# Projections of the local attentions: a reordered pipeline, the rotation's sum on GpSimd, one pipeline over both rows

## The chip, the cores and the metric

The kernel runs on one core of a Trainium2 chip. The metric is the device time of one execution in microseconds (us). A core has five engines that run their own instruction streams: TensorE (PE in the profile; its weight loads are PEld), VectorE (DVE), ScalarE (ACT), GpSimd (POOL), and SyncE (SP), which here only issues DMAs. They meet through semaphores. PSUM is what TensorE writes its sums to; SBUF is the on-chip memory that all engines read.

## The reference

Two transformer blocks over a batch of 2 rows of 2048 tokens with 256 features. The change touches one step of the last part, which runs twice (two layers). Cut to that step:

```
h = shift_token(x)                      # 4096 x 256: half of the features from the token before
q, k, v = split(h @ wqkv, 3)            # 256 x 1536
q = l2norm(q) * qs ; k = l2norm(k) * ks # per head, 8 heads of 64
q, k = rotary_xpos(q, k)                # q * cos*scale + rotate_half(q) * sin*scale, k with 1/scale
o = local_attention(q, k, v)            # windows of 128 tokens
```

The local attention and a gated unit follow; they aren't changed.

## The kernel before

The whole network is one program of stages with a barrier of all engines between them. `local_projections` (names I_... in the profile) is one such stage and runs twice. It takes the 32 tiles of 128 tokens (16 per row, `WIN` = 16, `B` = 2 rows) one after the other; u = tile mod 2 picks one of two buffers. For one tile n:

- SyncE loads the tile's tokens into `h` (two DMAs: the shifted half, L1553, and the other, L1554).
- *first*: TensorE transposes `h` into the PSUM tile `ph` (L1584). ScalarE copies `ph`, rounded, into `hhi` (L1625) and VectorE takes the rest, `hlo = ph - hhi` (L1679). Three products of such halves stand for one product in float32. `ph` is a single buffer.
- *mul*: TensorE does 18 matmuls (L1595): 12 into `pqk[u]` (q and k), then 6 into `pv`. ScalarE squares q and k (L1631, tile `sq`), copies v out (L1636) and takes the root of the sums (L1639). VectorE sums the squares (L1700, `ss`), clips the norm from below (L1707, on `nr`), inverts it (L1708, `rn`) and writes the normalised `qn` (L1709). SyncE stores v.
- *rotation*: GpSimd makes `t2`, the half with the sine, in two instructions of 128x512 (L1655). VectorE makes `t1 = qn * A` (L1687) and adds `t2` to it (L1691). `A` and `R` are tables (cosine and sine parts times the scale), made once at the start of the stage.
- *turn*: TensorE transposes the 128x1024 result in 8 pieces into `pt` (L1610), ScalarE copies that to `tT` (L1644), SyncE stores q and k (L1566).

Each engine's order is written out by hand in `skewed`: per row, tile n+1's *first* is issued inside tile n's *mul*, *turn* runs two tiles behind. VectorE rotates tile n-1 between the sum of squares and the clip of tile n. The loop `Fori(0, B)` runs the pipeline once per row, so it drains at the end of row 0 and fills again.

At the stage's start SyncE loads weights, tables, scales and an identity, in this order, then the first tokens. Everything waits for all four.

The views of the profile leave out buffer numbers, so `t1` and `t2` both read as I_t: L1655 writes t2, L1687 and L1691 write t1.

Of the kernel before, what the change touches and what calls it, by code (L numbers as in the profile page):

```python
# [1476 lines left out]
def local_projections(nc, sem, tag, xp, wqkv, tab, scales, ident, qT, kT, ve):  # L1477
# [5 lines left out]
    H = LD // 2  # L1483
    with ExitStack() as ctx:
# [36 lines left out]
        def skewed(eng, first, mul, turn):  # L1521


            M = WIN // 2
            with eng.Fori(0, B) as b:
                first(b, 0, 0, 0)
                mul(b, 0, 0, 0, (b, 1, 0, 1))
                mul(b, 1, 0, 1, (b, 2, 1, 0))
                with eng.Fori(0, M - 2) as m:
                    for u in range(2):  # L1530
                        mul(b, m * 2 + u + 2, m + 1, u, (b, m * 2 + u + 3, m + 1 + u, 1 - u))
                        turn(b, m * 2 + u, m, u)
                mul(b, WIN - 2, M - 1, 0, (b, WIN - 1, M - 1, 1))
                turn(b, WIN - 4, M - 2, 0)
                mul(b, WIN - 1, M - 1, 1, None)
                turn(b, WIN - 3, M - 2, 1)
                turn(b, WIN - 2, M - 1, 0)
                turn(b, WIN - 1, M - 1, 1)

        def nothing(*a):  # L1540
            pass

        @block.sync
        def _(sp):
            sp.dma_start(w[:], wqkv.rearrange("(kc p) n -> p kc n", p=P)).then_inc(c_in, 16)
            sp.dma_start(tb[:], tab.rearrange("(k w p) d -> p k w d", p=P, w=WIN)).then_inc(c_in, 16)
            sp.dma_start(sc[:].rearrange("p k d -> p (k d)"), scales.to_broadcast([P, 2 * LD])).then_inc(c_in, 16)
            sp.dma_start(idf[:], ident).then_inc(c_in, 16)

            def first(b, w_, m, u):  # L1550
                sp.wait_ge(t_done, b * WIN + w_ + 1)
                row = b * PADS + w_ * P
# [3 lines left out]
            def mul(b, w_, m, u, nxt):  # L1556
                if nxt:
                    first(*nxt)
                sp.wait_ge(v_done, b * WIN + w_ + 2)
                sp.dma_start(ve[ds(b * PADW + w_ * P + P, P), :], v[:, u].rearrange("p h e -> p (h e)")  # L1560
                             ).then_inc(v_out[u], 16)
# [6 lines left out]
            skewed(sp, first, mul, turn)  # L1568
# [5 lines left out]
        def _(pe):  # L1574
            for s in (t_done, v_mm, qt_done):
                pe.sem_inc(s, 1)
            pe.wait_ge(c_in, 64)
            pe.wait_ge(wlo_done, 2)

            def first(b, w_, m, u):  # L1580
                pe.wait_ge(h_in[u], b * (WIN // 2 * 32) + m * 32 + 32)
                pe.wait_ge(ht_done, b * WIN + w_ + 1)
# [4 lines left out]
            def mul(b, w_, m, u, nxt):  # L1587
                n = b * WIN + w_
# [12 lines left out]
                if nxt:  # L1601
                    first(*nxt)

            def turn(b, w_, m, u):
                n = b * WIN + w_
# [7 lines left out]
            skewed(pe, first, mul, turn)  # L1613

        @block.scalar
        def _(act):
            act.wait_ge(v_set, 2)
            act.wait_ge(c_in, 64)
            act.activation(whi[:], w[:], ACT.Copy).then_inc(whi_done, 1)

# [6 lines left out]
            def mul(b, w_, m, u, nxt):  # L1627
                n = b * WIN + w_
# [12 lines left out]
            def turn(b, w_, m, u):  # L1641
                act.wait_ge(qt_done, b * WIN + w_ + 3)
                act.wait_ge(qk_out[u], b * (WIN // 2 * 32) + m * 32 + 1)
                act.activation(tT[:, u].rearrange("p j g t -> p j (g t)"), pt[:], ACT.Copy).then_inc(ev_done, 1)  # L1644
            skewed(act, first, mul, turn)

        @block.gpsimd
        def _(pool):
            pool.wait_ge(tabs, 2)

            def mul(b, w_, m, u, nxt):

                pool.wait_ge(qn_done, b * WIN + w_ + 3)
# [5 lines left out]
            skewed(pool, nothing, mul, nothing)  # L1659

        @block.vector
        def _(dve):
            dve.wait_ge(c_in, 64)
            dve.sem_inc(qn_done, 1)
            dve.memset(v[:], 1.0).then_inc(v_set, 1)
            for j in range(2):
                dve.tensor_tensor(A[:, j], tb[:, 2 * j], sc[:, j:j + 1].to_broadcast([P, WIN, LD]), ALU.mult)
                for a, z in ((0, H), (H, 0)):
                    last = dve.tensor_tensor(R[:, j, :, a:a + H], tb[:, 2 * j + 1, :, a:a + H],
                                             sc[:, j:j + 1, z:z + H].to_broadcast([P, WIN, H]), ALU.mult)  # L1670
            last.then_inc(tabs, 1)
            dve.wait_ge(whi_done, 2)
            dve.tensor_tensor(wlo[:], w[:], whi[:].bitcast(F32), ALU.subtract).then_inc(wlo_done, 1)
            dve.wait_ge(tabs, 2)

            def first(b, w_, m, u):
                n = b * WIN + w_
# [19 lines left out]
            def mul(b, w_, m, u, nxt):  # L1697
                n = b * WIN + w_
# [736 lines left out]
```

## Time and profile before

| | us |
|---|---|
| median of 3 runs | 5195.83 |
| lowest, highest | 5181.3, 5202.37 |
| the profiled execution | 5158.03 |
| its span, first to last instruction | 5156.5 |
| the first of the two stages, first DMA issue to last | about 275 (3283 to 3558) |
| the second | about 280 (4199 to 4479) |

The span is 1.5 us under the time of the same execution. All durations below are from this one execution. A row of a timeline gives start, duration, engine, line, operation, output and inputs, and in brackets how long the engine had been idle and what released it. A duration includes any time in which the instruction was held by something inside the engine.

### The profile page before, as it was taken

The numbers are of one execution on the slowest core, as the hardware profiler recorded it, in microseconds if no ns is written. First come the engines' busy times: TensorE is split into PE (matmuls) and PEld (weight loads), VectorE is DVE, ScalarE is ACT, GpSimd is POOL, SyncE is SP. The second block draws the span as 40 slices with busy tenths as digits, with TensorE's granted clock in tenths as the row PEclk, the third lists the DMA queues.
The fourth block names the chain that finished last, engine by engine and source line by source line (L and its number), as shares of the span: only waits on it lengthen the run. The fifth ranks groups of instructions, "written<-read, shape, count | busy, mean of one in ns | idle before, by whom it ended". The sixth has DMA issues, their size and how long they took to land. (4 is left out here: it accounts for less than half of the span.)

```text
span 5156.5 us, 83448 instructions
## 1 busy us (share of the span) xinstructions
PE 4120.5 (80%) x25572; PEld 2739.7 (53%) x25572; DVE 3024.9 (59%) x5338; ACT 2489.3 (48%) x4335; POOL 1363.3 (26%) x2120
## 2 busy tenths in 40 slices
PE   4799999753999994659999996576996967699687
PEld 2444444343999992324444442454665755466465
DVE  1788878441444543748878783575563447656454
ACT  1377767612545541217767675233553423355343
POOL 1232323124000005011111111133882003388300
PEclk9699989976999997858979898798998989899898
DMA  7322322123121203361422221334451023444211
GB/s 227 40 33 33 51 35 33 45 101 108 49 88 49 70 31 119 123 115 26 64 43 45 43 45 64 109 120 142 155 156 51 28 57 115 147 148 156 73 37 37
DMA packets 327112, 413.90 MB, mean 80 GB/s; under 512 B 40772, under 2 KB 236225, under 8 KB 323196
## 3 DMA queue, kind: packets, MB, share of 16 engines
q1 hardware_dynamic: 278620, 257.43, 15.8%
q0 software_dynamic: 43552, 148.12, 13.5%
q8 instruction: 174, 2.85, 0.2%
q10 hardware_dynamic: 4608, 4.20, 0.2%
q14 instruction: 158, 1.29, 0.1%
HBM read 252.57 MB, written 156.19 MB: 79 GB/s over the span
## 5 line engine op out<-in xcount | busy, mean ns | idle before, releaser
L600 DVE TENSOR_REDUCE G_mpart<-G_pm 128x1 f32<-128x512 f32 (+3 forms) x1024 | 618.4, 651 | 209.6 <-PE G_pm L489 202.2
L600 DVE TENSOR_REDUCE B_mpart<-B_pm 128x1 f32<-128x512 f32 (+3 forms) x1024 | 618.1, 651 | 157.3 <-PE B_pm L489 149.3
L579 ACT ACTIVATE G_p<-G_psc 128x1024 f32<-128x1024 f32 (+1 forms) x576 | 532.9, 977 | 151.7 <-PE G_psc L526 149.9
L579 ACT ACTIVATE B_p<-B_psc 128x1024 f32<-128x1024 f32 (+1 forms) x576 | 532.2, 977 | 134.6 <-PE B_psc L526 132.8
L489 PE MATMUL G_pm<-G_ks,G_qs 48*128 48x512 f32 (+3 forms) x1664 | 466.3, 425 | 100.3 <-DMA G_ks<-G_one 58.4
L489 PE MATMUL B_pm<-B_ks,B_qs 48*128 48x512 f32 (+3 forms) x1664 | 453.7, 410 | 74.8 <-DMA B_ks<-B_one 42.5
L489 PEld LDWEIGHTS G_pm<-G_ks,G_qs 48*128 48x128 f32 x1664 | 253.0, 212 | 421.3 <-DVE G_mpart L600 210.7
L1786 POOL TENSOR_SCALAR J_pr<-J_pr,J_rc 128x256 f32<-128x256 f32 x512 | 462.8, 916 | 39.9 <-DVE J_rc L1924 37.5
L489 PEld LDWEIGHTS B_pm<-B_ks,B_qs 48*128 48x128 f32 x1664 | 241.8, 200 | 386.2 <-DVE B_mpart L600 218.7
L504 PE MATMUL G_po<-G_p,G_v 128*32 128x512 f32 (+3 forms) x2560 | 326.6, 592 | 0.1
L526 PE MATMUL G_psc<-G_qs,G_ks 50*128 50x512 f32 (+3 forms) x1280 | 307.0, 418 | 9.3 <-issue 6.8
L504 PE MATMUL B_po<-B_p,B_v 128*32 128x512 f32 (+3 forms) x2560 | 306.5, 562 | 1.2 <-POOL B_p L356 1.1
L1655 POOL TENSOR_TENSOR I_t<-I_qn,I_R 128x512 f32<-128x512 f32 x128 | 165.8, 1316 | 513.6 <-DVE I_qn L1709 513.6
L526 PE MATMUL B_psc<-B_qs,B_ks 50*128 50x512 f32 (+3 forms) x1280 | 292.3, 402 | 9.4 <-issue 6.8
L1141 ACT ACTIVATE E_hs<-E_pH,E_bf 128x384 f32<-128x384 f32 (+1 forms) x192 | 115.8, 603 | 346.6 <-PE E_pG L1094 346.3
L1094 PE MATMUL E_pH<-E_xT,E_wfg 128*128 128x384 f32 (+1 forms) x1152 | 252.5, 355 | 25.6 <-DVE E_wfg L1180 18.7
L1885 ACT ACTIVATE J_pr<-J_pS,J_nm 128x256 f32<-128x256 f32 x512 | 235.3, 479 | 38.0 <-DVE J_nm L1920 38.0
L1094 PE MATMUL E_pG<-E_xT,E_wfg 128*128 128x384 f32 (+1 forms) x1152 | 249.4, 352 | 0.0
L1107 PE MATMUL E_pO<-E_wp,E_a 128*128 128x256 f32 (+1 forms) x1920 | 234.6, 283 | 0.0
L1094 PEld LDWEIGHTS E_pH<-E_xT,E_wfg 128*128 128x128 f32 x1152 | 210.9, 191 | 36.5 <-issue 26.2
L1107 PEld LDWEIGHTS E_pO<-E_wp,E_a 128*128 128x128 f32 (+1 forms) x1920 | 230.0, 184 | 0.0
L1185 DVE SCALAR_TENSOR_TENSOR E_z<-E_pG,E_bg,E_hs 128x384 f32<-128x384 f32 (+1 forms) x192 | 123.6, 644 | 165.9 <-ACT E_hs L1141 164.8
(303 smaller groups left out, 7895.3 us busy)
## 6 DMA issues: line engine op xcount, KB each, us to landing
J_v<-lve SPq DMA_DIRECT2D x64, 520.0 KB, 3.8
J_k<-lkT SPq DMA_DIRECT2D x64, 512.0 KB, 4.9
lve<-I_v SPq DMA_DIRECT2D x64, 260.0 KB, 2.1
lqT<-I_tT SPq DMA_DIRECT2D x64, 256.0 KB, 2.4
lkT<-I_tT SPq DMA_DIRECT2D x64, 256.0 KB, 2.6
J_q<-lqT SPq DMA_DIRECT2D x64, 256.0 KB, 3.8
ein<-Z_z SPq DMA_DIRECT2D x8, 1228.0 KB
E_xin<-ein POOLq DMA_DIRECT2D x8, 1152.0 KB, 6.2
```

Of the source, the lines that this page charges most:

```text
L489: last = pe.matmul(t[:, n * w:(n + 1) * w], qs[s][rows, q // SUB, h // 2, q % SUB * P:(q % SUB + 1) * P], ks[s][rows, h // 2 % NA, first:f ...
L504: last = pe.matmul(po[VW * h:VW * (h + 1), off:CH], v[s][:, kb, h % nk], p[:, t % PSLOTS, h, at:at + CH - off], start=first[t], stop=final[t],
L526: score = pe.matmul(psc[:, h, at:at + CH - off], ks[s][rows, h // 2 % NA, kb * P:(kb + 1) * P], qs[s][rows, qc, h // 2, off:CH], start=Tru ...
L579: act.activation(p[:, t % PSLOTS, 2 * pr:2 * pr + 2, span(t)], psc[:, 2 * pr:2 * pr + 2, span(t)], ACT.Exp, scale=SC).then_inc(e_done[pr], 1)
L600: dve.tensor_reduce(mpart[:, heads[0] % 2, a:z, qb, kc], pm[slots[e]][:, 0:len(heads) * w].rearrange("p (h k) -> p h k", k=w), AX, ALU.max ...
L1094: last = pe.matmul(bank[ht % 2][:, 0:w], wfg_p[pw][:, i, kc, ht * P:(ht + 1) * P], xT[px][:, kc, 0:w], start=kc + j == 0, stop=kc == KC - ...
L1107: last = pe.matmul(pO[j // 2][0:r, j % 2 * D:(j % 2 + 1) * D], a[pa][:, ht, j * P:j * P + r], wp_p[pw][:, ht], start=j % 2 + ht + i == 0, ...
L1141: act.activation(hs[:, ht % 2, 0:w], pH[ht % 2][:, 0:w], ACT.Identity, bias=bf[:, s, ht:ht + 1]).then_inc(hs_done, 1)
L1185: dve.scalar_tensor_tensor(z[:, ht % 2, 0:w], pG[ht % 2][:, 0:w], bg[:, s, ht:ht + 1], hs[:, ht % 2, 0:w], ALU.add, ALU.mult).then_inc(z_d ...
L1655: last = pool.tensor_tensor(t2[:, u, :, :, a:a + H], qn[:, u, :, :, z:z + H], R[:, :, ds(w_, 1), a:a + H].to_broadcast([P, 2, LH, H]), ALU ...
L1786: last = pool.tensor_scalar(pr[:, u, pos(h)], pr[:, u, pos(h)], rc[:, u, pos(h):pos(h) + 1], None, ALU.mult)
L1885: last = act.activation(pr[:, u, pos(h)], pS[:, pos(h)], ACT.Exp, bias=nm[:, u, pos(h):pos(h) + 1], scale=8.0, accum_out=su[:, u, pos(h):p ...
```

## The change

In `local_projections` only (and the host's layout of the constant table, now one contiguous row per partition):

- Per tile n every engine now takes tile n+1's *first* ahead of tile n's *mul*: TensorE transposes `h` of tile n+1 before it projects tile n. ScalarE's and VectorE's orders follow: `hhi`, then square, v, root, `tT`; `hlo`, then t1 of tile n-1, sum of squares, clip, inverse, `qn` of tile n.
- SyncE loads tile n+2 in iteration n, as soon as `h[u]` was transposed.
- The sum `t1 + t2` is made by GpSimd (128x1024, its line L1707 of the changed kernel), behind its two products and VectorE's t1. GpSimd also makes the four pieces of the table `R`.
- The loops run over both rows: while row 0 ends, row 1's first tiles enter, with no drain between.
- At the start the weights come in two halves with a semaphore each, then identity, first tokens, scales, and the table last, by 128 long rows.

```diff
-            def skewed(eng, first, mul, turn):
...
         def _(sp):
-            sp.dma_start(w[:], wqkv.rearrange("(kc p) n -> p kc n", p=P)).then_inc(c_in, 16)
-            sp.dma_start(tb[:], tab.rearrange("(k w p) d -> p k w d", p=P, w=WIN)).then_inc(c_in, 16)
-            sp.dma_start(sc[:].rearrange("p k d -> p (k d)"), scales.to_broadcast([P, 2 * LD])).then_inc(c_in, 16)
-            sp.dma_start(idf[:], ident).then_inc(c_in, 16)
+            sp.dma_start(w[:, 0], wqkv[0:P, :]).then_inc(w_in[0], 16)
+            sp.dma_start(w[:, 1], wqkv[P:2 * P, :]).then_inc(w_in[1], 16)
+            sp.dma_start(idf[:], ident).then_inc(id_in, 16)
...
+            load(0, 0, 0, 0)
+            load(0, 1, 0, 1)
+            sp.dma_start(sc[:].rearrange("p k d -> p (k d)"), scales.to_broadcast([P, 2 * LD])).then_inc(tab_in, 16)
+            sp.dma_start(tb[:].rearrange("p k w d -> p (k w d)"), tab).then_inc(tab_in, 16)
...
+                with sp.Fori(1, M - 1) as m:
+                    for u in range(2):
+                        load_again(b, m * 2 + u + 2, m + (b * M + 1), u)
+                        v_store(b, m * 2 + u, m + b * M, u)
+                        qk_store(b, m * 2 + u - 2, m + (b * M - 1), u)
...
         def _(pe):
+                with pe.Fori(1, M - 1) as m:
+                    for u in range(2):
+                        take(b, m * 2 + u + 1, m + (b * M + u), 1 - u)
+                        project(b, m * 2 + u, m + b * M, u)
+                        turn(b, m * 2 + u - 2, m + (b * M - 1), u)
...
         def _(pool):
+            def rotate(b, w_, u):
+                n = w_ + b * WIN
+                pool.wait_ge(qn_done, n + 3)
                 for a, z in ((0, H), (H, 0)):
                     last = pool.tensor_tensor(
                         t2[:, u, :, :, a:a + H], qn[:, u, :, :, z:z + H],
                         R[:, :, ds(w_, 1), a:a + H].to_broadcast([P, 2, LH, H]), ALU.mult)
                 last.then_inc(t2_done, 1)
+                pool.wait_ge(t2_done, n + 3)
+                pool.wait_ge(t1_done, n + 2)
+                pool.tensor_tensor(t1[:, u], t1[:, u], t2[:, u], ALU.add).then_inc(r_done, 1)
...
         def _(dve):
             def rotate(b, w_, u):
...
-                dve.wait_ge(t2_done, n + 2)
-                dve.tensor_tensor(t1[:, u], t1[:, u], t2[:, u], ALU.add).then_inc(r_done, 1)
...
+            def normalise(b, w_, u):
...
+                link(dve.tensor_scalar(nr[:, u], nr[:, u], 1e-12, None, ALU.max), clip, n + 2)
...
+                with dve.Fori(1, M - 1) as m:
+                    for u in range(2):
+                        take(b, m * 2 + u + 1, 1 - u)
+                        rotate(b, m * 2 + u - 1, 1 - u)
+                        normalise(b, m * 2 + u, u)
```

VectorE, inside the loop over tiles. Before, one tile (L1700 sum of squares, L1679 `hlo`, L1687 t1, L1691 the sum, L1707 clip, L1709 `qn`):

```order
L1700 TENSOR_REDUCE I_ss<-I_sq 128x16
L1678 ISA
L1679 TENSOR_TENSOR I_hlo<-I_ph,I_hhi 128x256
L1685 REGISTER_ALU
L1686 REGISTER_ALU
L1687 ISA
L1687 TENSOR_TENSOR I_t<-I_qn,I_A 128x1024
L1691 TENSOR_TENSOR I_t<-I_t 128x1024
L1707 TENSOR_SCALAR I_nr<-I_nr 128x16
L1708 RECIPROCAL I_rn<-I_nr 128x16
L1709 TENSOR_TENSOR I_qn<-I_pqk,I_rn 128x1024
```

Of the change, one tile at the same place:

```order
L1724 TENSOR_TENSOR I_hlo<-I_ph,I_hhi 128x256
L1730 REGISTER_ALU
L1732 ISA
L1732 TENSOR_TENSOR I_t<-I_qn,I_A 128x1024
L1743 TENSOR_REDUCE I_ss<-I_sq 128x16
L1746 TENSOR_SCALAR I_nr<-I_nr 128x16
L1747 RECIPROCAL I_rn<-I_nr 128x16
L1748 REGISTER_ALU
L1749 TENSOR_TENSOR I_qn<-I_pqk,I_rn 128x1024
```

`hlo` and t1 now stand directly behind the `qn` of the tile before and ahead of the sum of squares; the addition is gone.

GpSimd, inside the loop over tiles. Before, one tile:

```order
L1653 ISA
L1655 ISA
L1655 TENSOR_TENSOR I_t<-I_qn,I_R 128x16x32
L1655 ISA
L1655 TENSOR_TENSOR I_t<-I_qn,I_R 128x16x32
```

Of the change:

```order
L1701 ISA
L1701 TENSOR_TENSOR I_t<-I_qn,I_R 128x16x32
L1701 ISA
L1701 TENSOR_TENSOR I_t<-I_qn,I_R 128x16x32
L1706 REGISTER_ALU
L1707 TENSOR_TENSOR I_t<-I_t 128x1024
```

The two products stay; the sum L1707 follows them (there is one such piece per tile), and it waits for the products and for VectorE's t1.

SyncE at the stage's start, of the change (before it was weights, tables 128x64x64, scales, identity, tokens):

```order
L1526 DMA I_w<-in_l_wqkv 128x1536
L1527 DMA I_w<-in_l_wqkv 128x1536
L1528 DMA I_idf<-in_ident 128x128
L1532 DMA I_h<-xp 128x128
L1533 DMA I_h<-xp 128x128
L1532 DMA I_h<-xp 128x128
L1533 DMA I_h<-xp 128x128
L1552 DMA I_sc<-in_l_scales 128x128
L1553 DMA I_tb<-in_xpos 128x4096
```

Tokens and identity moved ahead of the table, which is now the ninth issue.

## Rows read from the trace of the kernel before

**Rows 1.** Timeline, one tile in the middle of row 0 (start us, duration us).
```profile
3402.40 1.22 DVE L1709 TENSOR_TENSOR I_qn<-I_pqk,I_rn 128x1024 f32<-128x1024 f32 x1
3402.40 0.37 SPq L1553 DMA_DIRECT2D I_h<-xp  x1
...
3403.80 2.49 POOL L1655 TENSOR_TENSOR I_t<-I_qn,I_R 128x512 f32<-128x512 f32 x2 [4.51 <-DVE I_qn L1709]
...
3405.07 0.43 PE L1584 MATMUL I_ph<-I_idf,I_h 128*128 128x128 f32 x2 [0.97 <-DMA I_h<-xp]
...
3405.37 1.09 PE L1610 MATMUL I_pt<-I_idf,I_t 128*128 128x128 f32 x8
...
3406.04 0.42 DVE L1679 TENSOR_TENSOR I_hlo<-I_ph,I_hhi 128x256 fp32r<-128x256 f32 x1 [0.97 <-ACT I_hhi L1625]
3406.38 1.22 DVE L1687 TENSOR_TENSOR I_t<-I_qn,I_A 128x1024 f32<-128x1024 f32 x1
...
3406.50 1.03 ACT L1644 ACTIVATE I_tT<-I_pt 128x1024 f32<-128x1024 f32 x1
...
3408.37 0.38 SPq L1566 DMA_DIRECT2D lkT<-I_tT  x1
...
3409.17 0.37 SPq L1553 DMA_DIRECT2D I_h<-xp  x1
```

**Rows 2.** Timeline, the first tile of the stage.
```profile
3316.79 1.22 DVE L1700 TENSOR_REDUCE I_ss<-I_sq 128x16 f32<-128x1024 f32 x1 [5.66 <-ACT I_sq L1631]
...
3318.07 0.22 ACT L1639 ACTIVATE I_nr<-I_ss 128x16 f32<-128x16 f32 x1
3318.32 0.17 DVE L1707 TENSOR_SCALAR I_nr<-I_nr 128x16 f32<-128x16 f32 x1
...
3318.82 1.22 DVE L1709 TENSOR_TENSOR I_qn<-I_pqk,I_rn 128x1024 f32<-128x1024 f32 x1
```

**Rows 3.** Timeline, two places at the rows' ends where t1 meets t2.
```profile
3417.25 2.51 POOL L1655 TENSOR_TENSOR I_t<-I_qn,I_R 128x512 f32<-128x512 f32 x2 [4.09 <-DVE I_qn L1709]
...
3418.57 2.27 DVE L1687 TENSOR_TENSOR I_t<-I_qn,I_A 128x1024 f32<-128x1024 f32 x1
...
3542.96 3.51 POOL L1655 TENSOR_TENSOR I_t<-I_qn,I_R 128x512 f32<-128x512 f32 x2 [4.05 <-DVE I_qn L1709]
...
3544.15 1.22 DVE L1687 TENSOR_TENSOR I_t<-I_qn,I_A 128x1024 f32<-128x1024 f32 x1
```

**Rows 4.** GpSimd's only sum or product of 128x1024, by line (ns min/median/max).
```profile
L737 POOL TENSOR_TENSOR H_cx<-H_num,H_den x8: 2334/2348/2353, 3195.4 to 3260.6; 128x1024 f32<-128x1024 f32 x8
```

**Rows 5.** VectorE beside GpSimd's J_pr, local attention, by line (ns min/median/max).
```profile
L1920 DVE TENSOR_SCALAR J_nm<-J_mx x128: 169/275/533, 3582.9 to 4793.2; 128x4 f32<-128x4 f32 x128
...
L1924 DVE RECIPROCAL J_rc<-J_su x128: 171/178/180, 3585.8 to 4797.8; 128x4 f32<-128x4 f32 x128
...
L1786 POOL TENSOR_SCALAR J_pr<-J_pr,J_rc x512: 912/913/950, 3586.2 to 4803.2; 128x256 f32<-128x256 f32 x171
```

**Rows 6.** Timeline, the stage's DMA issues; then landing times of weights and of tables.
```profile
3283.34 0.41 SPq L1545 DMA_DIRECT2D I_w<-in_l_wqkv  x1
3283.96 0.83 SPq L1546 DMA_DIRECT2D I_tb<-in_xpos  x1
3284.84 11.60 SPq L1547 DMA_DIRECT2D I_sc<-in_l_scales  x1
...
DMA to landing us min/median/max: 6.4/6.4/6.5
...
DMA to landing us min/median/max: 15.3/15.4/15.4
```

**Rows 7.** Timeline, the end of the stage: last `qn`, last store.
```profile
3548.21 1.22 DVE L1709 TENSOR_TENSOR I_qn<-I_pqk,I_rn 128x1024 f32<-128x1024 f32 x1
...
3558.14 0.37 SPq L1566 DMA_DIRECT2D lkT<-I_tT  x1
```

**Rows 8.** Stretch: length, busy us (instructions) of PE, PEld, DVE, ACT, POOL; clock; DMA.
```profile
4345.00:4375.00 30.00, 18.94 (x70) 14.65 (x71) 10.38 (x15) 9.12 (x13) 2.94 (x3) 0.71 0.19 59
```

More of the change, by code:

```diff
@@ L1519, in local_projections @@
         block = ctx.enter_context(nc.Block())
-        def skewed(eng, first, mul, turn):
[L1524 to L1538, printed above, removed]
@@ L1553, in first, with load, v_store @@
+            sp.dma_start(w[:, 1], wqkv[P:2 * P, :]).then_inc(w_in[1], 16)
+            sp.dma_start(idf[:], ident).then_inc(id_in, 16)
+            def load(b, w_, q, u):
+                row = w_ * P + b * PADS
                 sp.dma_start(h[:, u, 0:P], xp[ds(row + 1, P), 0:P]).then_inc(h_in[u], 16)
                 sp.dma_start(h[:, u, P:D], xp[ds(row, P), P:D]).then_inc(h_in[u], 16)
[L1556 to L1560, printed above, removed]
+            def v_store(b, w_, q, u):
+                sp.wait_ge(v_done, w_ + b * WIN + 2)
+                sp.dma_start(ve[ds(w_ * P + (b * PADW + P), P), :], v[:, u].rearrange("p h e -> p (h e)")
@@ L1574, in _, with take @@
         def _(pe):
[L1575 to L1582, printed above, removed]
+            pe.wait_ge(id_in, 16)
+            def take(b, w_, q, u):
+                pe.wait_ge(h_in[u], q * 32 + 32)
+                pe.wait_ge(ht_done, w_ + b * WIN + 1)
                 for kc in range(KC):
@@ L1600, in mul, with turn @@
                 last.then_inc(v_mm, 1)
[L1601 to L1605, printed above, removed]
+            def turn(b, w_, q, u):
+                n = w_ + b * WIN
                 pe.wait_ge(r_done, n + 2)
@@ L1658, in mul, with take @@
                 last.then_inc(t2_done, 1)
-            skewed(pool, nothing, mul, nothing)
+                pool.wait_ge(t2_done, n + 3)
+                pool.wait_ge(t1_done, n + 2)
+                pool.tensor_tensor(t1[:, u], t1[:, u], t2[:, u], ALU.add).then_inc(r_done, 1)
+            for b in range(B):
+                with pool.Fori(0, M) as m:
+                    for u in range(2):
+                        rotate(b, m * 2 + u, u)
         @block.vector
         def _(dve):
-            dve.wait_ge(c_in, 64)
-            dve.sem_inc(qn_done, 1)
             dve.memset(v[:], 1.0).then_inc(v_set, 1)
[L1666 to L1677, printed above, removed]
+            for kc in range(KC):
+                dve.wait_ge(whi_done, 2 + kc)
+                dve.tensor_tensor(wlo[:, kc], w[:, kc], whi[:, kc].bitcast(F32), ALU.subtract).then_inc(wlo_done, 1)
+            def take(b, w_, u):
+                n = w_ + b * WIN
                 dve.wait_ge(hi_done, n + 2)
@@ L1711, in mul @@
                                   rn[:, u].unsqueeze(2).to_broadcast([P, NB, LD]), ALU.mult).then_inc(qn_done, 1)
-            def turn(b, w_, m, u):
-                if isinstance(w_, int) and w_ == WIN - 3:
-                    rotate(b, WIN - 1, 1)
-            skewed(dve, first, mul, turn)
+            take(0, 0, 0)
+            dve.wait_ge(tab_in, 32)
+            for j in range(2):
+                last = dve.tensor_tensor(A[:, j], tb[:, 2 * j], sc[:, j:j + 1].to_broadcast([P, WIN, LD]), ALU.mult)
+            last.then_inc(a_tab, 1)
+            dve.wait_ge(a_tab, 2)
+            for b in range(B):
+                for u in range(2):
+                    take(b, 1 + u, 1 - u)
+                    if u:
+                        rotate(b, 0, 0)
+                    elif b:
+                        rotate(b - 1, WIN - 1, 1)
+                    normalise(b, u, u)
+                with dve.Fori(1, M - 1) as m:
+                    for u in range(2):
+                        take(b, m * 2 + u + 1, 1 - u)
+                        rotate(b, m * 2 + u - 1, 1 - u)
+                        normalise(b, m * 2 + u, u)
+                take(b, WIN - 1, 1)
+                rotate(b, WIN - 3, 1)
+                normalise(b, WIN - 2, 0)
+                if b < B - 1:
+                    take(b + 1, 0, 0)
+                rotate(b, WIN - 2, 0)
+                normalise(b, WIN - 1, 1)
+            rotate(B - 1, WIN - 1, 1)
 def local_attention(nc, sem, tag, qT, kT, ve, wo, masks, ident_bf, ident, X, xp):
```

137 lines of the change are left out of this document (92 added, 45 removed).

## The prediction

> **What bounds the kernel now.** I read three views: the timeline of one tile, the collisions of VectorE with GpSimd, and the start and end of the stage. The busy shares of the whole span say little: the changed stage is two stretches of 275 and 280 us out of 5156.5, so everything but those stays as it is.
>
> In the middle of a row a tile takes 6.8 us (load to load, 3402.40 to 3409.17 [rows 1]). No engine is full in it. The circle is: SyncE issues the load at 3402.40, TensorE waits 0.97 us for it and transposes at 3405.07, then does the turn of an older tile (3405.37, 1.09 us), ScalarE copies that to `tT` (3406.50, 1.03), SyncE issues two stores, the second at 3408.37, and only then the next load. SyncE's order puts the load behind the stores, so the DMA's latency stands in every tile. TensorE's work is at most 6.77 - 0.97 = 5.8 us per tile.
>
> From the first tile's `qn` (ends 3318.82 + 1.22 = 3320.04 [rows 2]) to the last one's (3549.43 [rows 7]) there are 31 steps in 229.4 us, 7.40 each: the drain and refill between the rows cost the rest. From there to the end of the last store issue (3558.51) are 9.1 us.
>
> **Part 1, the head.** SyncE's table DMA keeps the next issue for 11.60 us, and tables land 15.4 us after their issue at 3283.96 [rows 6]. After the change w, w, identity, four token loads and scales go first; at 0.6 us an issue (3283.34 to 3283.96) the table starts at 3288.1. It is 2.1 MB, the weights are 1.57 MB and land in 6.4 us, so I take 6.4 x 2.1 / 1.57 = 8.6 us and land it at 3296.7 (call it L). The weights then need copies and one tile's matmuls, which I put some 1 us earlier than the way over the tables. The tables are now made by both engines: VectorE's two parts (like t1, 1.22 each [rows 1]) and GpSimd's four (half of t2's 2.49, so 1.25 each). By [rows 3], below, these exclude each other: VectorE, GpSimd, VectorE, GpSimd gives VectorE free at L + 3.5. Then `hlo` 0.4, sum of squares 1.2, root 0.3, clip (held until GpSimd's third part ends, L + 5.9) and 1.55 to the end of `qn`: L + 7.5 = 3304.2 instead of 3320.04. **Gain 15.9 us per stage**; 8 to 19 for an L that is later or earlier.
>
> **Part 2, the loads.** Loaded one iteration ahead and no longer behind the stores of this one, they leave the circle. The 0.97 us and the stores' issue are hidden by TensorE's 18 matmuls.
>
> **Part 3, the rotation.** This decides. What must be known is which instructions of VectorE and GpSimd exclude each other. In [rows 3] t1 (two inputs in SBUF) starts at 3418.57 inside t2's second half and takes 2.27 instead of 1.22: it ends 1.08 after GpSimd's 3417.25 + 2.51. At the other place t1 starts first by a hair (3544.15) and takes 1.22, and t2 takes 3.51 instead of 2.5, ending 1.10 behind t1. So they exclude each other, in order of asking, per instruction. The sum of squares, `hlo` and `qn` have at most one SBUF tensor of size and run beside t2 at their normal length (the sum ran inside 3403.80 to 3406.29 in every tile). The clip is another kind of instruction, TENSOR_SCALAR from SBUF to SBUF. It never meets GpSimd here before. The nearest row is J_nm, the same kind, which lies beside GpSimd's J_pr and takes 169 to 533 ns, while the reciprocal of the same size beside the same J_pr stays at 171 to 180 [rows 5]. So a clip is held by GpSimd and an inverse isn't.
>
> GpSimd's sum of 128x1024 is not in the trace; the same operation and size is L737, 2.35 us [rows 4]. That is its low bound as well as my value; nothing suggests less.
>
> Now one tile by the new order, from the end of `qn` as 0. t2 starts at 0.18 (3403.62 to 3403.80 [rows 1]), its first half ends at 1.43. `hlo` starts 0.08 before `qn` ends (as t1 does behind `hlo`), t1 asks 0.34 later, at 0.26: too late by under 0.1 us. It waits for the first half and ends at 1.43 + 1.08 = 2.51; t2's second half ends 1.10 later, 3.61. The sum follows on GpSimd at about 3.75 and ends at **6.10**. VectorE meanwhile: sum of squares 2.43 to 3.65, and from its end to the clip's start 0.31 (3318.01 to 3318.32 [rows 2]), so the clip asks at 3.96, 0.2 us behind the sum. It is held until 6.10, is done 0.06 later, and from a clip's end to the end of `qn` are 1.55 (3318.49 to 3320.04). The next `qn` ends at **7.7**. GpSimd was done at 6.10, so the next tile begins alike: this repeats itself. TensorE (5.8) and ScalarE (0.4 + 1.03 + 0.6 + 0.2 + 1.03 = 3.3) have room in 7.7.
>
> So the addition that leaves VectorE comes back as a wait behind it. 31 steps x (7.7 - 7.4) = **+9.3 us** per stage, though the boundary between the rows has gone and is in that 7.4. If the second half of t2 beat the waiting t1, t1 would end at 3.7, the sum still at about 6.1: the same. Bounds for the step: 7.6 with every handoff at its shortest, 7.9 with 0.2 more on GpSimd.
>
> **Part 4, the tail.** Behind the last `qn` the sum costs 2.35 in place of 1.2: **+1.1**. The turn, `tT` and stores stay.
>
> **Sum:** -15.9 + 9.3 + 1.1 = -5.5 per stage, -11 for both. The profiled execution's 5158.0 would be 5147; the median of the three runs lies 38 us above that execution, and I take the difference from the median: 5195.8 - 11 = **5185**. Own range: (-19 + 6.2 + 1.1) x 2 = -23 to (-8 + 15.5 + 1.1) x 2 = +17, so 5173 to 5213. A median of three repeats to about 0.5%, 26 us, so this is "no change".
>
> The Trainium skill (SBUF — State Buffer, Who interferes with whom) says that a GpSimd instruction and a VectorE one with two SBUF inputs, or a tensor_scalar in a mode with both ports, hold the shared ports for a whole instruction and the other fully blocks. For t1 the trace agrees (2.27 against 1.22). For the clip the rows are weaker than the rule: J_nm is never held for more than 533 - 169 = 364 ns, beside instructions of 913 ns. By the rule the step is 7.7 as above; with 364 ns at most the clip would go through at 4.3 and `qn` end at 5.9, under 6.10, and that is the first rival.
>
> **The rivals.**
>
> *B, the other order holds (0.30).* If once t1 asks while GpSimd is still in the sum before, it goes first: from the sum's end as 0, t1 ends at 1.08, t2 at 2.18 and 3.43, the sum at 3.55 to 5.9. VectorE: sum of squares to 2.2, clip asks at 2.5, held to 3.43, `qn` ends at 5.05, t1 asks at 5.3, before 5.9. This repeats itself as well, and with 0.6 us to spare, where the forecast's order has less than 0.1 (t1 at 0.26, t2 at 0.18). The step is 5.9, bound by GpSimd's 4.85 + t1, just over TensorE's 5.8. It comes about if the clip isn't held to the end, or if GpSimd is late once by 0.1 us: at the head it has the last part of `R` until about L + 7.2, against `qn` at L + 7.5. Against it: the handoffs repeat to 0.1 us in [rows 1, 2]. Time: 31 x (5.9 - 7.4) = -46.5, with head and tail -61.3 per stage, -123: 5073.
>
> *B', a part of the tiles in each order (0.14).* It may flip in the code between the loops, where tile 14 or 15 is. Half of the tiles: 31 x (6.8 - 7.4) = -18.6, -33 per stage, -67: 5129.
>
> *C, TensorE's clock (0.10), slower than before.* At 7.7 us a tile TensorE pauses twice, about 1 us each. Around the old boundary, with 18.9 of 30 us busy, the granted clock was 0.71 [rows 8], a mix of its 2.4 and 1.2 GHz levels. In the forecast it is busy about 5.5 of 7.7 us, 0.7, hardly more than there. At 1.2 GHz its 5.8 become about 11.6, 3.9 over the step. It decides from (26 + 11) / 3.9, some 10 of the 62 steps. With a third of the tiles: 21 x 3.9 = +82, less 11: 5267. Against it: the pauses are short ones between bursts of 4 us, and that stretch had pauses of 5 us.
>
> *D, the head gives nothing,* if table and weights share the DMA queues worse than I think: +32 on the forecast at most, 5217, just past its own range and still within 0.5%; it has no chance of its own.
>
> **How the numbers follow.** Forecast 0.46, B 0.30, B' 0.14, C 0.10. Faster by over 0.5% are B and B': 0.44; same 0.46; slower 0.10. The range goes from 5065 (B, with the handoffs of the step at their shortest) to 5213; C is left out.
>
> **What would show it.** Right: in the middle of a row `qn` follows `qn` by 7.6 to 7.9 us, alike in both rows; the clip takes over 2 us instead of 0.17 and ends with GpSimd's sum; t1 takes 2.2 to 2.3; the sum takes 2.35; no load stands as the releaser of a transpose; the first `qn` ends some 21 us after the first DMA issue, not 37. Wrong: clips of under 0.6 us, or t1 directly behind a sum with t2 at 3.5 for its two halves and a step of 5.9; a granted clock under 0.9 in the stage.

## The result and the profile after

| | before | the change |
|---|---|---|
| median of 8 runs each, us | 5185.69 | 5148.02 |
| lowest to highest | 5169.93 to 5202.37 | 5129.97 to 5165.06 |
| ratio | | 0.9926, 95% interval 0.9903 to 0.9949 |
| the profiled execution, us | 5158.03 | 5155.78 |
| granted clock over the span | 0.887 | 0.885 |
| stage 1 / stage 2, first DMA issue to the end of the last | 275.2 / 279.8 | 249.3 / 272.7 |

The change is 38 us faster. The forecast was 5185; 5148 lies in the range of 5065 to 5213, but past the bound of 0.5% in which the forecast's own case stood. The 5185 was the median of three runs, 5195.8, less 11; with the median of eight above, the same -11 gives 5175. So the number to hold against the forecast's -11 is -38. A second timing of the same kernel, beside the experiments, gave 0.9932 (0.9908 to 0.9956).

The two profiled executions differ by 2 us only. The two stages are 33.0 us shorter in the second, and unchanged code took 30.8 us longer in it: 17.9 ahead of the stages (the first weight DMA goes out at 3301.19, where [rows 6] has 3283.34) and 20.5 behind them, less 7.6 between them. Hence only the stages are compared below, and medians of repeats for the whole.

Timeline of the changed kernel, one tile in the middle of row 0 (start us, duration us, engine, line, operation, tiles, shapes, in brackets the idle time before and its releaser), answering to [rows 1]:

```profile
3369.67 1.23 DVE L1749 TENSOR_TENSOR I_qn<-I_pqk,I_rn 128x1024 f32<-128x1024 f32 x1
...
3369.88 0.41 SPq L1533 DMA_DIRECT2D I_h<-xp  x1
...
3370.81 0.41 DVE L1724 TENSOR_TENSOR I_hlo<-I_ph,I_hhi 128x256 fp32r<-128x256 f32 x1
3371.08 3.48 POOL L1701 TENSOR_TENSOR I_t<-I_qn,I_R 128x512 f32<-128x512 f32 x2 [1.85 <-DVE I_qn L1749]
3371.14 2.27 DVE L1732 TENSOR_TENSOR I_t<-I_qn,I_A 128x1024 f32<-128x1024 f32 x1
...
3371.95 0.43 PE L1584 MATMUL I_ph<-I_idf,I_h 128*128 128x128 f32 x2 [1.58 <-DMA I_h<-xp]
...
3373.34 1.20 DVE L1743 TENSOR_REDUCE I_ss<-I_sq 128x16 f32<-128x1024 f32 x1
...
3374.72 2.39 POOL L1707 TENSOR_TENSOR I_t<-I_t 128x1024 f32<-128x1024 f32 x1 [0.16 <-POOL I_t L1701]
...
3374.82 2.32 DVE L1746 TENSOR_SCALAR I_nr<-I_nr 128x16 f32<-128x16 f32 x1 [0.28 <-ACT I_nr L1657]
...
3377.46 1.22 DVE L1749 TENSOR_TENSOR I_qn<-I_pqk,I_rn 128x1024 f32<-128x1024 f32 x1
```

From `qn` to `qn` are 7.79 us (3369.67 to 3377.46). t1 asks 0.06 us behind t2 and takes 2.27. A clip of 128 x 16 numbers asks 0.10 behind the sum and takes 2.32: it ends at 3377.14, with the sum (3377.11). This is the forecast's order, called A from here. In stage 1 it doesn't last. The timeline at tile 17 of the first stage, the second tile of row 1, VectorE and GpSimd:

```profile
3455.24 1.23 DVE L1749 TENSOR_TENSOR I_qn<-I_pqk,I_rn 128x1024 f32<-128x1024 f32 x1
...
3456.71 1.23 DVE L1732 TENSOR_TENSOR I_t<-I_qn,I_A 128x1024 f32<-128x1024 f32 x1
...
3456.96 3.37 POOL L1701 TENSOR_TENSOR I_t<-I_qn,I_R 128x512 f32<-128x512 f32 x2 [2.08 <-DVE I_qn L1749]
```

`qn` ends at 3456.47. GpSimd begins 0.49 us later, where it took 0.17 to 0.20 in the 17 tiles before, so t1 (at 3456.71) goes first and takes its plain 1.23. From there to the end of the stage the other order, rival B's, holds. Timeline, VectorE and then GpSimd, one such tile:

```profile
3490.57 1.23 DVE L1749 TENSOR_TENSOR I_qn<-I_pqk,I_rn 128x1024 f32<-128x1024 f32 x1
...
3492.04 1.83 DVE L1732 TENSOR_TENSOR I_t<-I_qn,I_A 128x1024 f32<-128x1024 f32 x1
3493.79 1.21 DVE L1743 TENSOR_REDUCE I_ss<-I_sq 128x16 f32<-128x1024 f32 x1
3495.28 1.01 DVE L1746 TENSOR_SCALAR I_nr<-I_nr 128x16 f32<-128x16 f32 x1 [0.28 <-ACT I_nr L1657]
...
3496.70 1.22 DVE L1749 TENSOR_TENSOR I_qn<-I_pqk,I_rn 128x1024 f32<-128x1024 f32 x1
```
```profile
3490.38 2.41 POOL L1707 TENSOR_TENSOR I_t<-I_t 128x1024 f32<-128x1024 f32 x1 [0.16 <-POOL I_t L1701]
3492.74 3.50 POOL L1701 TENSOR_TENSOR I_t<-I_qn,I_R 128x512 f32<-128x512 f32 x2
3496.33 2.40 POOL L1707 TENSOR_TENSOR I_t<-I_t 128x1024 f32<-128x1024 f32 x1
```

Here t1 waits for the sum that runs (ends 3492.79), then works before GpSimd's products; these start at once behind the sum in the record, are 1.0 longer than 2.5, and end at 3496.24. The clip waits for them only (1.01), and gets through ahead of the next sum. GpSimd has no idle time left, and steps alternate between 5.85 and 6.13 (3490.57 to 3496.70).

The second stage stays in order A up to its last step. That one is 5.18: no `hlo` is left to stand in front of its t1, which then asks 0.04 behind `qn`, 0.15 ahead of GpSimd, and is not held. The clip by line, in the stretches 3318:3458, 3458:3548 and 4198:4450 (count, busy us, mean ns, idle before):

```profile
L1746 DVE TENSOR_SCALAR I_nr<-I_nr 128x16 f32<-128x16 f32 x18 | 39.2, 2180 | 5.1 <-ACT I_nr L1657 5.1
...
L1746 DVE TENSOR_SCALAR I_nr<-I_nr 128x16 f32<-128x16 f32 x14 | 14.0, 1000 | 4.0 <-ACT I_nr L1657 4.0
...
L1746 DVE TENSOR_SCALAR I_nr<-I_nr 128x16 f32<-128x16 f32 x32 | 69.8, 2182 | 9.0 <-ACT I_nr L1657 9.0
```

The head of the first stage, and its end, answering to [rows 2, 6, 7] (timeline, and the landing time of the table):

```profile
3301.19 0.35 SPq L1526 DMA_DIRECT2D I_w<-in_l_wqkv  x1
...
3305.50 0.43 SPq L1553 DMA_DIRECT2D I_tb<-in_xpos  x1
...
3316.64 3.43 DVE L1756 TENSOR_TENSOR I_A<-I_tb,I_sc 128x1024 f32<-128x1024 f32 x2 [5.27 <-DMA I_tb<-in_xpos]
...
DMA to landing us min/median/max: 11.1/11.2/11.2
...
3538.43 1.22 DVE L1749 TENSOR_TENSOR I_qn<-I_pqk,I_rn 128x1024 f32<-128x1024 f32 x1
...
3549.95 0.51 SPq L1543 DMA_DIRECT2D lkT<-I_tT  x1
```

The first `qn` ends at 3324.01, 22.8 us after the first issue. Put beside before, with the same three cuts (first issue, first `qn`, last `qn`, end of the last store issue):

| us, stage 1 / stage 2 | before | the change | difference |
|---|---|---|---|
| head, to the end of the first `qn` | 36.7 / 40.1 | 22.8 / 22.9 | -13.9 / -17.2 |
| 31 steps | 229.4 / 230.7 | 215.6 / 239.0 | -13.8 / +8.3 |
| tail | 9.1 / 9.1 | 10.8 / 10.8 | +1.7 / +1.7 |
| together | 275.2 / 279.8 | 249.3 / 272.7 | -25.9 / -7.1 |

### The profile page after: what moved, and what is told of

Read it like the earlier page. It is cut to its first block and busy times, and to the rows that moved or that the text cites. A ratio compares the mean times of both kernels' runs of the same rounds, so it can differ in the third digit from the quotient of the medians.

```text
span 5154.3 us, 82911 instructions
## 1 busy us (share of the span) xinstructions
PE 4152.3 (81%) x25572; PEld 2767.8 (54%) x25572; DVE 3103.4 (60%) x5268; ACT 2483.8 (48%) x4334; POOL 1586.5 (31%) x2192
## 5 line engine op out<-in xcount | busy, mean ns | idle before, releaser
L1701 POOL TENSOR_TENSOR I_t<-I_qn,I_R 128x512 f32<-128x512 f32 x128 | 223.1, 1764 | 85.9 <-DVE I_qn L1749 85.9
L1981 DVE TENSOR_REDUCE J_mx<-J_pS 128x4 f32<-128x1024 f32 x128 | 156.7, 1224 | 116.1 <-PE J_pS L1898 115.2
```

Of the source, the lines that this page charges most:

```text
L1701: last = pool.tensor_tensor(t2[:, u, :, :, a:a + H], qn[:, u, :, :, z:z + H], R[:, :, ds(w_, 1), a:a + H].to_broadcast([P, 2, LH, H]), ALU ...
L1981: dve.tensor_reduce(half(mx[:, u], j), half(pS, j), AX, ALU.max).then_inc(m_done, 1)
```

## The experiments

The questions: is the clip's hold the cause of the slow step; does the order of t1 and t2 decide it; and why did stage 1 leave order A at tile 17? All kernels are shown against the changed one, except where it says before. "Stage" is the time from the first DMA issue to the end of the last, as above.

**1. The change once more, unaltered.**

> The changed kernel once more, unchanged, for its profile. My theory: a tile takes either 7.8 us (order A: GpSimd starts its products before VectorE asks for t1, and the clip is held behind the sum) or 6.0 us (order B: t1 asks while GpSimd is still in the sum before). The two keep themselves up, and only a delay of GpSimd by 0.1 us or more carries it from A to B, so the steps will again be 7.7 to 7.9 or 5.8 to 6.1 and nothing between, and the tile of the turn to B may be another one than tile 17 of the first stage. Rival: the turn belongs to the code at tile 16 (the loop over the second row starts there), then it stands at tile 17 of the first stage again and never in the second.

One run, 5145.9 us. Stage 1 had again 17 steps of order A and turned at tile 17; stage 2 was in A up to its last step; stages 249.2 and 272.8. The expected two periods came, and of the place of the turn the rival was right: it isn't chance, but belongs to tile 17 of the first stage.

**2. t1 ahead of the rest term.** VectorE issues t1 of tile n-1 before `hlo` of tile n+1, so that it asks about 0.3 us earlier.

```diff
 # VectorE, inside the loop
-    take(b, m * 2 + u + 1, 1 - u)
     rotate(b, m * 2 + u - 1, 1 - u)
+    take(b, m * 2 + u + 1, 1 - u)
     normalise(b, m * 2 + u, u)
```

> VectorE's t1 of the tile before is issued ahead of hlo instead of behind it, 0.34 us earlier, so it asks before GpSimd starts its products. By the theory of the two orders that alone puts all tiles into B: step 6.0 us in both stages (31 x 6.0 = 186 us from the first qn to the last), clips of 1.0 us or less in place of 2.3; against the profiled run of the change (17 + 31 steps of 7.8) some 87 us less, so about 5065 and 0.977 of before. Rival (GpSimd's load or the clip is the limit in any order): the step stays at 7.8, 5150. Rival (hlo later holds TensorE up): 6.3 to 6.6, 5090.

5062.69 us, ratio 0.979 (0.9736 to 0.9844). Stages 217.1 and 219.3. Timeline, VectorE and then GpSimd:

```profile
3402.84 1.22 DVE L1749 TENSOR_TENSOR I_qn<-I_pqk,I_rn 128x1024 f32<-128x1024 f32 x1
3404.10 2.03 DVE L1732 TENSOR_TENSOR I_t<-I_qn,I_A 128x1024 f32<-128x1024 f32 x1
...
3407.87 0.68 DVE L1746 TENSOR_SCALAR I_nr<-I_nr 128x16 f32<-128x16 f32 x1 [0.28 <-ACT I_nr L1657]
...
3408.88 1.23 DVE L1749 TENSOR_TENSOR I_qn<-I_pqk,I_rn 128x1024 f32<-128x1024 f32 x1
```
```profile
3402.65 2.40 POOL L1707 TENSOR_TENSOR I_t<-I_t 128x1024 f32<-128x1024 f32 x1 [0.16 <-POOL I_t L1701]
3405.01 3.51 POOL L1701 TENSOR_TENSOR I_t<-I_qn,I_R 128x512 f32<-128x512 f32 x2
3408.60 2.40 POOL L1707 TENSOR_TENSOR I_t<-I_t 128x1024 f32<-128x1024 f32 x1
```

Nothing of the work was taken away, only the order of two instructions swapped; the steps are 6.04 here and the clip 0.68. GpSimd's rows join each other: it is the bound.

One step did not come out as expected, the first of stage 2 (7.80). Timeline:

```profile
4173.00 1.23 DVE L1732 TENSOR_TENSOR I_t<-I_qn,I_A 128x1024 f32<-128x1024 f32 x1
...
4176.93 2.29 DVE L1746 TENSOR_SCALAR I_nr<-I_nr 128x16 f32<-128x16 f32 x1 [0.28 <-ACT I_nr L1657]
```
```profile
4176.79 2.40 POOL L1707 TENSOR_TENSOR I_t<-I_t 128x1024 f32<-128x1024 f32 x1 [0.16 <-POOL I_t L1701]
```

Here t1 went first and took its plain 1.23, but the clip asked 0.14 behind GpSimd's sum and was held for 2.29. So the clip's hold alone makes a step of 7.8, with t1 not held at all. A later profile of this kernel (10) has the same first step (7.79).

**3. The clip away.** ScalarE's root gets a bias of 1e-24 instead, and the inverse reads it directly. The clip's lower bound is thereby replaced by a bias, which is another computation for norms near zero.

```diff
-    act.activation(nr[:, u], ss[:, u], ACT.Sqrt).then_inc(nr_done, 1)
+    act.activation(nr[:, u], ss[:, u], ACT.Sqrt, bias=tiny[:]).then_inc(nr_done, 1)
...
-    link(dve.tensor_scalar(nr[:, u], nr[:, u], 1e-12, None, ALU.max), clip, n + 2)
```

> The clip instruction is gone; ScalarE's root has a bias of 1e-24 in its place, which gives the same least norm. If the clip held behind GpSimd's sum is what makes 7.8, qn ends at 5.4 after the one before, t1 then asks before the sum has ended at 6.15, and all steps but the first are 6.0 us: about 5065. The inverse, now in the clip's place, must stay at 0.25 us beside GpSimd's sum. Rival (any small VectorE instruction that reads and writes SBUF is held): the inverse takes 2.3 us and the step stays 7.7, 5150.

5062.3 us, ratio 0.9799 (0.9758 to 0.984); stages 218.4 and 218.0. Timeline, VectorE:

```profile
3403.08 0.25 DVE L1748 RECIPROCAL I_rn<-I_nr 128x16 f32<-128x16 f32 x1 [0.37 <-ACT I_nr L1658]
...
3404.93 2.56 DVE L1734 TENSOR_TENSOR I_t<-I_qn,I_A 128x1024 f32<-128x1024 f32 x1
```

The inverse has the clip's shape and stands in its place (GpSimd works from 3400.44 to 3403.93), and takes 0.25. So it isn't the size, nor the place, but the kind of instruction. `hlo` and t1 keep the changed kernel's order, and order A doesn't come about at all. By itself that doesn't show that the clip's hold makes the 7.8, because the start changed too: without the clip the first `qn` ended while GpSimd was still at its table, so the first t1 (3298.52) was already ahead of GpSimd's products (3298.77), and experiment 4 shows that such a start is enough. That order A couldn't last without the hold is an estimate from the changed kernel's rows: the t1 at 3378.94 would ask some 2.15 us earlier (2.32 less 0.17), at 3376.8, before the sum's end at 3377.11.

**4. GpSimd late once.** One product of 128x512 more ahead of GpSimd's loop.

```diff
+    last = pool.tensor_tensor(t2[:, 1].rearrange("p j h e -> p (j h) e")[:, :, 0:H], tb[:, 3, :, H:LD],
+                              sc[:, 1:2, 0:H].to_broadcast([P, WIN, H]), ALU.mult)
```

> One more instruction on GpSimd, once per stage, ahead of its loop: a product of 128x512 into a buffer that nothing reads, 1.25 us. It adds work. By the theory of the two orders GpSimd is then still busy when the first t1 is asked for, t1 goes first, and all 31 steps of both stages are 6.0 us: about 5065, 0.977 of before. Rival (the orders don't keep themselves up, or another thing than GpSimd's lateness turned them): 7.8 again from the second or third tile on, 5150.

5074.7 us, ratio 0.9813 (0.9769 to 0.9857); stages 218.9 and 217.9, all 62 steps from 5.84 to 6.14, the clips at 1.0 (0.54 in the first tile). 1.30 us more work at the start of each stage saves some 30 and 55 us: both orders carry themselves on, and the start picks one.

**5. The sum back on VectorE, everything else changed.**

```diff
 # VectorE, directly behind t1
+    dve.wait_ge(t1_done, n + 2)
+    dve.wait_ge(t2_done, n + 3)
+    dve.tensor_tensor(t1[:, u], t1[:, u], t2[:, u], ALU.add).then_inc(r_done, 1)
```

> The change with only the sum given back to VectorE, directly behind t1. Then no GpSimd sum holds a clip, but VectorE waits for GpSimd's second product at 3.6 us after qn, adds to 4.9, sums the squares from 4.8, clips at 6.3 and ends qn at 8.05: step 8.0 to 8.1 in all tiles of both stages, with t1 still 2.3 and clips of 0.17; about 5199. Rival (the sum on GpSimd is itself the cost of the 7.8): a step under 7, 5130 or less.

5221.55 us in one run, against 5177.77 (median of 7) of before; stages 282.4 and 282.7, steps 8.04 to 8.18 as expected. The stages explain 10 us of the loss; the rest is within what one run can differ. The clip is back at 0.18. Timeline, VectorE:

```profile
3398.53 2.27 DVE L1729 TENSOR_TENSOR I_t<-I_qn,I_A 128x1024 f32<-128x1024 f32 x1
3402.02 1.23 DVE L1734 TENSOR_TENSOR I_t<-I_t 128x1024 f32<-128x1024 f32 x1 [1.22 <-POOL I_t L1701]
...
3404.66 0.18 DVE L1746 TENSOR_SCALAR I_nr<-I_nr 128x16 f32<-128x16 f32 x1 [0.28 <-ACT I_nr L1657]
```

In the new order VectorE now waits for t2's end instead (1.22 idle, and 1.05 inside t1), in a chain with nothing beside it. Of the change's parts this pairing matters: the new order needs the sum on GpSimd.

**6. Before, with only the sum on GpSimd**, and **7. before, with only the loads two tiles ahead of the stores.**

```diff
 # 6: GpSimd, behind its two products; VectorE's addition is dropped
+    pool.wait_ge(t2_done, b * WIN + w_ + 3)
+    pool.wait_ge(rot, b * WIN + w_ + 2)
+    pool.tensor_tensor(t1[:, u], t1[:, u], t2[:, u], ALU.add).then_inc(r_done, 1)
 # 7: SyncE
+    first(b, m * 2 + u + 4, m + 2, u)
+    store(b, m * 2 + u + 2, m + 1, u)
+    turn(b, m * 2 + u, m, u)
```

> The kernel before with only the sum moved to GpSimd (and the waits that this needs). There t1 stands behind the sum of squares and hlo, when the products are done, and the clip follows t1 at once, 0.1 us ahead of the GpSimd sum, so it isn't held: clips of 0.2 us, sum 2.35, and the step stays with the load's circle at 6.8 to 6.9. Two drains per stage get 1.2 us longer: about 5191, no change. Rival (the sum on GpSimd costs wherever it stands): clips of 1 to 2 us and a step of 7.5 or more, 5220.

> The kernel before with only SyncE's order changed: tile n+2 is loaded in iteration n. If the load's latency is what sets 6.9 us in the middle of a row, the transposes no longer wait for a DMA and the step falls to the 6.55 to 6.65 that the first tiles of a row have, where t1 meets GpSimd's second product: 24 steps per stage x 0.3, 15 us for both, 5171. Rival (VectorE's chain of 5.7 us plus waits sets it): 6.9 stays.

6, one run: 5176.97 us against 5177.77, stages 277.5 and 279.3. Steps 6.7 to 7.2 in the middle of a row, clips 0.17: in before's order the clip asks 0.16 us ahead of GpSimd's sum (3407.66 and 3407.82). 7, one run: 5184.44 where 5171 was expected, stages 272.6 and 275.3. Its steps are 6.70 in the middle of a row, not 6.55 to 6.65; over the 30 steps within rows the mean falls from 6.89 and 6.80 in before to 6.77 and 6.67. So neither part alone brings much: -2.6 and -4.5 us from the loads, +2.3 and -0.5 from the sum. How long an engine sat idle for the load of `h` (us, times), by tile, in the stretch 3330:3400, in 7 not at all; in the kernel before and then in the changed kernel:

```profile
  DMA I_h<-xp: 10.2, 10
```
```profile
  DMA I_h<-xp: 12.0, 8
...
DMA to landing us min/median/max: 1.8/2.1/2.3
```

In 7 the load has left the circle, and the step is only 0.1 us shorter: VectorE's sum then waits 1.25 us for t2's second half in each tile (at 3407.84), and that sets the step next. In the changed kernel the load has not left.

**8. Both: no clip, and t1 first.**

> t1 ahead of hlo and no clip instruction together. In order B the clip's wait of 1.0 us is hidden, since VectorE waits for the end of GpSimd's sum anyway, and the limit is GpSimd's 2.5 + 1.1 + 2.4: step 5.9 to 6.0 as with each edit alone, about 5065, not less. If the held clip still counts in order B, the step falls under 5.8.

5074.31 us, ratio 0.9782 (0.9718 to 0.9845); stages 217.6 and 217.1. Like 2 and 3: with either mended, the other has nothing left to give, since GpSimd is full.

**9. GpSimd's tile loop as one piece of code.** The change has the loop written out twice, once for each row, and tile 17 is the second tile of the second copy.

```diff
-            for b in range(B):
+            with pool.Fori(0, B) as b:
                 with pool.Fori(0, M) as m:
```

> The change with one edit: GpSimd's two written-out copies of its tile loop (one for each row) become one copy inside a loop over the rows, so that the whole stage runs the same instructions. Theory: the turn of stage 1 at tile 17, the first pair's second half of row 1's copy, comes from that second copy being run for the first time, which made GpSimd's products begin 0.50 us instead of 0.18 us behind the normalised tile; with one copy nothing is new at tile 17, t1 never gets ahead, and both stages stay at steps of 7.7 to 7.85 us. Stage 1's sum of steps is then 239 us instead of 215.6, and the time about 23 us over the change's, near 5170 us. Rival: the delay has another source (a fetch that belongs to the place in time, or the DMA traffic); then the stage still turns, at tile 17 or another, and the time stays within 10 us of 5148. A second rival: the extra loop level makes GpSimd's address arithmetic slower in every step by 0.1 us or more, t1 gets ahead everywhere, and both stages run at 5.9 us a step, near 5070 us.

5140.14 us in one run, where the change, timed beside it, had 5177.75 (11); stages 273.8 and 219.9. Stage 1 is now in order A to the end: tile 17 passes at steps of 7.8. Stage 2, however, is in order B from its first step. Timeline of its first tile, VectorE and then GpSimd:

```profile
4245.26 1.22 DVE L1749 TENSOR_TENSOR I_qn<-I_pqk,I_rn 128x1024 f32<-128x1024 f32 x1
...
4246.73 1.22 DVE L1732 TENSOR_TENSOR I_t<-I_qn,I_A 128x1024 f32<-128x1024 f32 x1
```
```profile
4244.87 1.29 POOL L1692 TENSOR_TENSOR I_R<-I_tb,I_sc 128x512 f32<-128x512 f32 x1
4246.72 3.61 POOL L1701 TENSOR_TENSOR I_t<-I_qn,I_R 128x512 f32<-128x512 f32 x2 [0.56 <-DVE I_qn L1749]
```

By the recorded starts GpSimd is 0.01 us ahead of t1, and t1 still wins (1.22 long). In the changed kernel the same place has t2 ahead by 0.05, and it wins:

```profile
4206.41 3.52 POOL L1701 TENSOR_TENSOR I_t<-I_qn,I_R 128x512 f32<-128x512 f32 x2 [0.52 <-DVE I_qn L1749]
...
4206.46 2.31 DVE L1732 TENSOR_TENSOR I_t<-I_qn,I_A 128x1024 f32<-128x1024 f32 x1
```

So the turn at tile 17 goes away with the second copy of the code, in this one run, and the time that the theory forecast (5170) was missed because stage 2 turned in its own way: a start 0.04 us later by GpSimd's way into the loop picks the other order for 31 tiles. That GpSimd is late in a copy that runs for the first time is not shown: in the changed kernel the second tile of the first copy, and tile 17 of stage 2 in yet another copy, were at their first run too and not late (0.19 and 0.19 behind `qn`). The second rival, slower address arithmetic in every step, is out, since stage 1 stayed in A.

**10, 11. The better version and the change, timed together.**

> The version of the change in which VectorE issues t1 of tile n - 1 ahead of the rest term of tile n + 1, timed in five rounds beside the change itself. Both stages should again take 217 to 219 us, steps of 5.84 to 6.13 us, and the ratio to the kernel before should lie between 0.975 and 0.982, 1.1 to 1.8 per cent under that of the change timed in the same call.

> The change unaltered, in five rounds beside the version with t1 first. It should give a ratio of 0.990 to 0.995 again, with stage 1 turning to steps of 5.85 and 6.12 us at tile 17 and stage 2 at 7.8 us throughout, as in both earlier profiles.

t1 first: 5077.7 us, ratio 0.9748 (0.9706 to 0.979), a hair under the expected 0.975, and 1.9% under the change, where 1.1 to 1.8 was expected; stages 217.8 and 219.2. The change: 5177.75, ratio 0.9932 (0.9908 to 0.9956); stages 248.7 and 272.7, turning at tile 17 again. Swapping two instructions is worth 100 us, 1.9%, by these medians. The stages account for 84 of them (521.4 less 437.0); the rest is within the spread of the repeats.

How full GpSimd is in this version (stretch, length, busy us of PE, PEld, DVE, ACT, POOL, granted clock, DMA share, GB/s):

```profile
3330.00:3510.00 180.00, 162.34 (x831) 130.49 (x829) 163.94 (x181) 90.41 (x148) 176.21 (x92) 1.00 0.48 150
```

## Why the prediction came out as it did

**The head** (forecast -15.9 a stage) gave -13.9 and -17.2. The table was issued a little earlier than assumed (4.3 us behind the first issue, not 4.8) but landed after 11.1 us, not 8.6. The size was right: in the trace its packets run from 3307.48 to 3316.27, 8.8 us. But they began 2.0 us after the issue, when the last of the weights' packets had ended (3307.31); the first weights, with nothing ahead of them, began 1.0 us after theirs (3302.19). L was 15.4 us after the first issue and not 13.4. From L to the end of `qn` were 7.4, where 7.5 was forecast. In stage 2, before had a longer head (40.1), which I hadn't looked up; the two errors cancel by luck: -31.1 in all against -31.8.

**The loads.** This step failed, at no cost in time. TensorE still waits for them, for 12.0 us in 8 tiles (experiment 7's view). The load of the tile transposed at 3371.95 was issued at 3369.88, 2.07 us before, which is a landing time: SyncE's order puts it ahead of this iteration's stores but behind those of the iteration before, and these wait for the rotation, which is now late. So a load "one iteration ahead" stands behind the same stores as before. It costs nothing in order A, where the clip's hold sets the step, nor in order B, where GpSimd is full. Where the loads do leave (7), 0.1 us a step is all that it brings.

**The rotation, order A** was right in its mechanism and nearly in its size: 7.7 forecast, 7.8 measured, t1 2.27 (2.25), the sum 2.39 (2.35, the row of another stage), the clip 2.2 to 2.3 and ending with the sum. Stage 2 shows the whole term: +8.3 against +9.3. Two small errors nearly cancel in it: 30 steps were 7.8 and not 7.7, and the last one, which the forecast took for a step like the others, was 5.18. That the clip's hold makes the slow step is shown by the timeline and by the first step of stage 2 in experiment 2, where the clip was held and t1 was not; that the order of two requests picks the period, by 2 and 4. Rival B's price was right too: -123 by the rows, and in experiment 2 the stages are 118.6 us shorter than before.

The Trainium skill (SBUF — State Buffer, Who interferes with whom) has a tensor_scalar in a mode with both ports held for whole GpSimd instructions. No run shows which mode the clip is in, but for its hold they agree, with 2.3 us against 0.17 without GpSimd, where the weaker row J_nm [rows 5] allowed at most 364 ns beside instructions of 913. The trace of before shows why it was weaker: of the 84 J_nm that take over 190 ns, 28 end within 0.08 us behind the end of the J_pr beside them, but 56 already end 0.49 to 0.58 us after its start. So GpSimd's TENSOR_SCALAR of 128x256 lets VectorE in once on its way, and the sum of 128x1024 doesn't. (In the forecast's first rival, a clip held for 364 ns puts the end of `qn` at 6.04 and not 5.9; that is still under 6.10.)

**What failed is that order A repeats itself to the end.** I had written that it has under 0.1 us to spare, where B has 0.6, and that handoffs repeat to 0.1 us. The repeating itself was even better than assumed: in the 47 tiles in which order A held, GpSimd began 0.17 to 0.20 us behind `qn` and t1 asked 0.24 to 0.26. But GpSimd was late by 0.3 us once, at tile 17 of stage 1, and there was no way back: 14 steps in order B. That is rival B' (part of the tiles in each order, chance 0.14), at another tile than I named and with 14 of 62 steps, not half. With A to the end, stage 1's steps would be about 239 as in stage 2, 23.4 more, and the stages together 10 us shorter than before and not 33: the forecast's -11. So the case was B', the size between it and the forecast. That the time still lies in the range owes to the range, which reached down to B, and not to the forecast's case.

**The tail** took +1.7 instead of +1.1. The sum costs what was forecast (2.34 in place of 1.23), but the last `qn` now ends at 3539.65, while GpSimd is still in the sum before; its products start at 3540.55, 0.9 later, where they started 0.08 later before.

**The clock.** Rival C did not come about. Granted was 0.94 in the stretch in order A and 0.98 in the one in order B:

```profile
3330.00:3450.00 120.00, 92.98 (x437) 72.32 (x435) 114.13 (x95) 45.09 (x77) 89.45 (x47) 0.94 0.38 118
3460.00:3540.00 80.00, 70.24 (x356) 55.37 (x354) 74.77 (x81) 39.38 (x65) 78.31 (x41) 0.98 0.48 151
```

TensorE is busy for 0.77 of the time in order A, where I reckoned 0.7. The clock did give a little: cut into stretches of 20 us, order A has 0.91 to 1.00, where before has 1.00 in the middle of its rows. But the steps are 7.8 throughout, in the stretches at 0.91 and in those at 1.00, so it cost nothing here.

**Still open:** what in GpSimd's second copy of the code took the 0.3 us at tile 17. The trace puts it between two register instructions in front of the first product, 0.37 us apart there, 0.07 in the tiles of order A and at most 0.15 in any other. Experiment 9, one run, shows that it goes away with the copy. That it is the fetching of instructions run for the first time is only argued, and two other first runs speak against it (9).

## What to carry to other kernels

Where two engines exclude each other on a shared resource, lay out one period of the loop by order of asking, for each order that can hold itself, and give each its period; then ask by how much the one that you expect is ahead. A margin under 0.1 us over 60 repeats is too thin to forecast from: the kernel should be written so that the better order wins by a wide margin (here t1 in front of a short instruction that needs nothing of GpSimd: 1.9% of the time). And before work is moved to a second engine, see which small instructions on the critical path that engine can hold: a clip of 128 x 16 numbers took 2.3 us there, longer than the addition that had been moved away (1.2).

## What the runs showed of the hardware that wasn't expected

- Of two small VectorE instructions of one shape (128x16) beside the same GpSimd work, TENSOR_SCALAR is held (0.17 to 2.34 us), RECIPROCAL is not (0.25 or 0.26 in all 64 tiles of every kernel whose profile is told of here).
- GpSimd's hold ends between two of its instructions: a waiting VectorE instruction goes in between them, though GpSimd's next is ready (t1 at 3492.04, 1.83, between the sum and the products).
- The order of asking counts to a few hundredths: by the recorded starts, t2 ahead of t1 by 0.05 us won, by 0.01 us lost (one case).
- GpSimd's TENSOR_SCALAR of 128x256 (0.91 us) holds a VectorE TENSOR_SCALAR for a part of its time only (56 of 84 held ones ended 0.49 to 0.58 us after its start).
- A kernel can settle into one of two periods, 7.8 or 6.0 us a tile, and stay there; a delay of 0.3 us, or of 0.04 at the start, chose. It repeated in each of the three profiles of the changed kernel.
